# Self-attention of layer 3: partner halves by a VectorE shuffle instead of permutation products

## The reference

```python
cos, sin = _rope_tables(L, x.dtype)                  # L = 32, HEAD_DIM = 16, 16 heads
def _rotate_half(x):
    x1, x2 = (x[..., :HEAD_DIM // 2], x[..., HEAD_DIM // 2:])
    return jnp.concatenate([-x2, x1], axis=-1)
q = q * cos + _rotate_half(q) * sin
k = k * cos + _rotate_half(k) * sin
scores = jnp.einsum('bhqd,bhkd->bhqk', q, k) / sqrt(hd)
out = jnp.einsum('bhqk,bhkd->bhqd', softmax(scores), v)
x = x + out @ o_w.T + o_b                            # q, k, v are projections of the layer norm of x
```

## Time and profile before

| | us |
|---|---|
| median of 3 runs (3510.6 to 3521.19) | 3512.74 |
| profiled execution, its span | 3512.3 |
| of it the self-attention of layer 3, first to last instruction (2203.68 to 2332.94) | 129.3 |
| one turn of its loop | 7.06 |

### The profile page before, as it was taken

One profiled execution on the slowest core, in us unless ns is written; L12 is line 12 of the kernel. 1 busy time (PEld: TensorE's weight loads), 2 busy tenths in 40 slices (PEclk: granted clock), 3 DMA queues, 4 the chain that ended last, 5 costly groups with the idle time before them and its releaser, 6 DMA issues. The chain is left out here.

```text
span 3512.3 us, 105565 instructions
## 1 busy us (share of the span) xinstructions
PE 3266.2 (93%) x39150; PEld 2585.9 (74%) x39150; DVE 2217.2 (63%) x7505; ACT 1454.0 (41%) x4212; POOL 1003.2 (29%) x1620
## 2 busy tenths in 40 slices
PE   7978999999987999999999999888999999988799
PEld 6767887777766888888877777765666777767576
DVE  4767226666667988889556666763334666668455
ACT  2334335555532333333255555541111555556222
POOL 0112113333243444444323333442110111112421
PEclk9989999999997999999999999979999999999699
DMA  6643332222112000000011111042112111110323
GB/s 222 212 177 154 115 100 58 57 57 54 62 40 103 3 2 2 2 2 2 13 44 45 43 43 44 2 146 98 46 46 69 43 39 39 39 35 2 114 79 113
DMA packets 145872, 225.26 MB, mean 64 GB/s; under 512 B 14216, under 2 KB 121480, under 8 KB 143816
## 3 DMA queue, kind: packets, MB, share of 16 engines
q1 hardware_dynamic: 138816, 203.16, 18.4%
q0 software_dynamic: 6816, 18.69, 1.5%
HBM read 201.03 MB, written 38.74 MB: 68 GB/s over the span
## 5 line engine op out<-in xcount | busy, mean ns | idle before, releaser
L3303 POOL TENSOR_TENSOR l1fu_second_weighed<-l1fu_second,l1fu_parts 128x256 bf16<-128x256 bf16 x384 | 273.0, 739 | 342.9 <-DVE l1fu_second L3544 336.0
L3355 PEld LDWEIGHTS l1fu_ps_u<-l1f_xnT_all,l1f_key_in 128*128 128x128 f32 x2048 | 252.5, 195 | 17.4 <-issue 11.2
L3355 PE MATMUL l1fu_ps_u<-l1f_xnT_all,l1f_key_in 128*128 (+1 forms) x2048 | 255.0, 279 | 8.7 <-issue 5.5
L3366 PE MATMUL l1fu_ps_y<-l1f_key_out,l1fu_units 128*128 128x256 f32 x1024 | 250.6, 389 | 1.7 <-DVE l1fu_units L3552 1.7
L3366 PEld LDWEIGHTS l1fu_ps_y<-l1f_key_out,l1fu_units 128*128 128x128 f32 x1024 | 185.7, 190 | 33.3 <-issue 6.0
L3417 ACT COPY l1fu_plane<-l1fu_ps_p 128x512 f32<-128x512 f32 x128 | 75.1, 586 | 249.4 <-PE l1fu_ps_p L3345 249.4
L3539 DVE TENSOR_TENSOR l1fu_first<-l1fu_index,l1fu_counted 128x1024 bf16<-128x1024 bf16 x128 | 165.0, 1289 | 20.3 <-PE l1fu_ps_p L3345 17.6
L3425 ACT ACTIVATE l1fu_units<-l1fu_ps_u 128x512 f32<-128x512 f32 x128 | 76.6, 599 | 150.6 <-PE l1fu_ps_y L3366 138.5
L3011 DVE TENSOR_TENSOR l2f_hidden<-l2f_hidden,l2f_ps_u 128x512 f32<-128x512 f32 x55 | 37.8, 688 | 148.9 <-PE l2f_ps_u L2755 139.1
L1020 ACT ACTIVATE l2x_scores<-l2x_scores,l2x_minus_big 128x257 f32<-128x257 f32 x256 | 129.2, 513 | 2.5 <-DVE l2x_minus_big L1104 2.4
L1020 ACT ACTIVATE l1x_scores<-l1x_scores,l1x_minus_big 128x257 f32<-128x257 f32 x256 | 129.2, 513 | 2.1 <-DVE l1x_minus_big L1104 2.1
(11 more groups left out here) (747 smaller groups left out, 8379.8 us busy)
## 6 DMA issues: line engine op xcount, KB each, us to landing
rows_by_expert<-in_zeros_dram SPq DMA_DIRECT2D x1, 17544.0 KB
l0x_ctxT<-in_ctx_T_dram SPq DMA_DIRECT2D x32, 514.0 KB, 5.2
l0x_ctx_rows<-in_ctx_dram SPq DMA_DIRECT2D x64, 256.0 KB, 3.4
l0f_w<-in_L_ffn_w_dram SPq DMA_DIRECT2D x16, 1024.0 KB, 5.1
l1x_ctx_sb<-in_ctx_T_dram SPq DMA_DIRECT2D x64, 256.0 KB, 2.8
l2x_ctx_sb<-in_ctx_T_dram SPq DMA_DIRECT2D x64, 256.0 KB, 2.8
l3x_ctx_sb<-in_ctx_T_dram SPq DMA_DIRECT2D x64, 256.0 KB, 2.8
l1x_mask_raw<-in_mask_int_dram SPq DMA_DIRECT2D x16, 514.0 KB, 3.9
```

The source lines that it names most:

```text
L3303: last = nc.gpsimd.tensor_tensor(second_weighed[:, k % 2, part], second[:, k % 2], parts[:, 1 - par, part, TC * k:TC * k + TC].unsqueeze(2 ...
L3355: last = nc.tensor.matmul(ps_u[:, k % 2, j, :], key_in[:, c, JS * k + j, :], xnT_all[:, c, bass.ts(tile, P)], start=(c == 0), stop=(c == C ...
L3366: last = nc.tensor.matmul(ps_y, units[:, k, j, :], key_out[:, JS * k + j, :], start=(k + j == 0), stop=(k == K - 1 and j == JS - 1))
```

## The change

The partner halves come from VectorE. Its instruction `stream_shuffle` copies a tile and takes, inside each group of 32 partitions, each output partition from the input partition that a list of 32 names; here p XOR 8. `swap_halves` shuffles `kraw` into `krot` and `qT` into `qrot` at the end of VectorE's turn i, behind `normed`, and signals `rot_ready`, for which `rotate_keys` on GpSimd and `spread_queries` of the next turn wait as before. `rotated`, `keep_rotated`, the bank `ps_qkr` and the matrix `other_half` (64 KB of the table of constants) are gone. The values have their own bank as in the other layers, and the two waits between scores and values are gone.

```diff
-        "other_half": p[:, None] == (p ^ (HD // 2))[None],
...
-        if rope:
-            ps_qkr = ps("ps_qkr", [P, 2, C, P])
-            ps_v = ps_s[:, 0, P:P + D]
-        else:
-            ps_v = ps("ps_v", [P, 512])[:, 0:D]
+        ps_v = ps("ps_v", [P, 512])[:, 0:D]
...
+        other_half = [p ^ (HD // 2) for p in range(32)]
...
             def scores(n, slot):
-                if rope:
-                    pe.wait_ge(s["v_spread"], n)
...
-            def rotated(n, slot):
-                after(pe, s["rot_ready"], n - 1)
-                pe.wait_ge(s["qT_ready"], n)
-                pe.wait_ge(s["kraw_ready"], n)
-                for a, raw in enumerate((qT[:, slot], kraw[:])):
-                    for c in range(C):
-                        last = nc.tensor.matmul(ps_qkr[:, a, c, :], core.table("other_half"), raw[:, c, :], start=True,
-                                                stop=True)
-                last.then_inc(s["qkr_ready"], 1)
...
             def values(n, slot):
-                if rope:
-                    after(pe, scores_read, n - 1)
...
-                if rope and there(i, QA):
-                    rotated(i + QA + 1, (par + QA) % 2)
...
-            def keep_rotated(n):
-                act.wait_ge(s["qkr_ready"], n)
-                after(act, s["kT_ready"], n - 1)
-                after(act, s["q_spread"], n - 1)
-                nc.scalar.copy(rot[:], ps_qkr[:]).then_inc(s["rot_ready"], 1)
...
-                if rope and there(i, QA):
-                    keep_rotated(i + QA + 1)
...
+            def swap_halves(n, slot):
+
+                after(dve, s["kT_ready"], n - 1)
+                wait(dve, s["kraw_ready"], n)
+                nc.vector.stream_shuffle(krot, kraw[:], other_half)
+                after(dve, s["q_spread"], n - 1)
+                wait(dve, s["qT_ready"], n)
+                nc.vector.stream_shuffle(qrot, qT[:, slot], other_half).then_inc(s["rot_ready"], 1)
...
                     normed(dve, nc, s, i + XA + 2, core.x[:, i + XA + 1, :], xn[:], mean[:], rstd[:])
                 if is_turn(i, -XA):
                     fill()
+                if rope and there(i, QA):
+                    swap_halves(i + QA + 1, (par + QA) % 2)
```

More of the change, by code:

```diff
@@ L235, in ps @@
             return ctx.enter_context(nc.psum_tensor(f"{tag}_{name}", shape, F32))
-        s = semaphores(nc, tag, LN_SEMS + """ turned xnT_ready qk_ready qkr_ready v_ready
+        s = semaphores(nc, tag, LN_SEMS + """ turned xnT_ready qk_ready v_ready
             qT_ready kraw_ready rot_ready k_turned kT_ready q_spread v_spread scores_ready biased_ready
```

## The result

Twelve runs of the changed kernel have a median of 3529.26 us, against 3512.59 us for twelve runs of the kernel before beside them. The ratio is 1.0042 with an interval of [1.0029, 1.0054], a loss of 14.8 us (10 to 19). I had put most on no measurable change (0.53) and 0.41 on slower; slower it is. By the ratio on the announced 3512.74 us the time is 3527.5 us, just inside my range of 3511 to 3528; the median itself lies 1.3 us above its top. My own forecast was 9.3 us, 3522. The profiled execution lasts 3527.9 us, 15.6 us more than the one of before.

A forecast was written before the change was run, and what follows sets the result against it. A closed VectorE-TensorE loop was taken as the bound, with TensorE in it only from transposes to output product. Thirteen shuffle pairs at s = 0.88 us, 11.4 us, less 2.1 gave 9.3 us, 3522 us; range 3511 to 3528.

The forecast's parts named there:

- rival A: VectorE's two shuffles don't overlap with neighbours: s = 1.0 to 1.24 us, 3524 to 3527 us; chance 0.32.
- the forecast's own range: With s from 0.64 to 1.0 us and the lag gain up to 0.2 us: 3517 to 3524 us.
- The loop: Third layer's self-attention: a turn is a closed loop over VectorE and TensorE, links summing to 7.08 us.
- D: TensorE, 96% busy in the loop, is the bound: 10 to 13 us come back, about 3501 us; chance 0.05.
- B: Only VectorE's own work counts in the loop: 6.85 us a turn, about -2 us, 3511 us; chance 0.10.
- s: Time the two shuffles put between `xn` and the next reciprocal on VectorE: 0.88 us, bounds 0.64 and 1.24 us.
- The gain of 0.10 us from `mixed` to the transposes: TensorE reaches its waits sooner in the loop: 0.31 to 0.21 us a turn, bounds nothing and 0.2 us.
- 13 s - 2.1: Sum over loop, unrolled turns, tail and constants: 9.3 us slower with s at 0.88 us.
- s - 0.35: Turns before tile 1's: second shuffle pair costs s, but the first scores start some 0.35 us earlier.
- The tail: Turns after the loop: shuffles for tiles 12 and 13 partly absorbed by waiting for TensorE, costing s - 0.6.
- The smaller table of constants: Table 64 KB smaller of 515.5 KB, load of 3.7 us: up to 0.46 us gained, counted as -0.15.
- rival C: TensorE's clock falls to 0.5 as it pauses; 3.5 us from transposes to add double, +35 us or more; chance 0.03.

The follow-up runs named there:

- e1: Changed kernel plus eight unread TensorE products where the permutation products were; 3524.64 us, ratio 1.0045 to the kernel before.
- e11: The kernel with eight unread TensorE products added to the changed kernel, unchanged, measured again on another occasion; 3518.89 us, ratio 1.0028 to the kernel before.
- e4: Kernel before with only the values in their own bank and without the two waits between scores and values; 3515.76 us, ratio 1.0011.
- e10: Changed kernel with shuffles and bias addition behind `mixed`, queries and keys behind TensorE's output product, no unread products; 3508.78 us, ratio 1.0001 to the kernel before.
- e2: Changed kernel without the keys' shuffle, the queries' shuffle cut to two elements; 3522.64 us, ratio 1.0030 to the kernel before.
- e9: Changed kernel with shuffles and GpSimd's bias addition moved behind `mixed`, plus eight unread TensorE products; 3513.15 us, ratio 1.0011 to the kernel before.
- e6: Changed kernel with shuffles moved behind `mixed`, plus eight unread TensorE products; 3517.72 us, ratio 1.0017 to the kernel before.
- e12: The changed kernel again, unchanged, on the chip of e9 and e10; 3524.46 us, ratio 1.0044 to the kernel before.

## Why the prediction was right in part, and what failed

- **The range.** That the time lies in it is luck. Most of its upper part stood there for rival A, dearer shuffles, and the forecast's own range ended at 3524. The shuffles were cheaper than the working value; what carried the time to 3527.5 us was the clock, which the range left out.
- **The loop.** Right. The links of the changed kernel at full clock add up to the measured 7.76 us with the one new link of 0.68 us, the removed products, ScalarE's copy and GpSimd were in no link, and D and B fell: taking TensorE's work away gave nothing back, in e1 putting it back gained.
- **s, 0.88 us.** Mis-sized; it measured 0.68 us, close to the lower bound of 0.64. A shuffle takes 0.44 us, as worked out from the transposes, but the load of the list that I added at 0.07 us costs nothing. Rival A, no overlap, is out with it, though the time lies only just above its 3524 to 3527 us. The estimate from the Trainium skill's "The perf-mode tier table" ("VectorE: DVE Perf Modes"), 0.53 us a shuffle, was further off; the measurement decides.
- **The gain of 0.10 us from `mixed` to the transposes.** Mis-sized, about 0.03 us a turn on the mean of the ten. It was read from one turn, and the lag depends on the parity: in the changed kernel's loop it is 0.31 us in one turn (`mixed` ends at 2256.08, the transposes start at 2256.39) and 0.21 us in the next (2263.84 to 2264.05). Before, the same two turns have 0.31 to 0.35 and 0.25 to 0.28 us. In the written-out turn ahead of the loop it is 0.06 us, before and after.
- **The sum without the clock.** With the measured s, 13 s - 2.1 gives 6.7 us, 3519 us. e1 has the sublayer at 136.2, e11 at 138.9 us, 5.7 and 8.4 us over before. For the loop alone 10 x (0.68 - 0.03) = 6.5 us, and e1 has 77.06 - 70.56 = 6.5 us. For the turns ahead of the first reciprocal the sum had s - 0.35 = 0.33 us; measured is 0.1 us, less than their scatter. The tail absorbed more than said (the four turns behind the loop are 0.6 us shorter than before, not s - 0.6 longer), and e4, which changes the bank of the values alone, has the same 0.6 us there; I had the bank at nothing. The smaller table of constants landed after 3.2 instead of 3.7 us, and the first statistics start at 4.9 instead of 5.2 us, 0.3 us where I had 0.15.
- **The step that failed: the clock, rival C at 0.03.** I priced it as all or nothing, 1.2 GHz for all of the 3.5 us from the transposes to the add in every turn, +35 us, and so rare. It came as 3.3 us at 1.2 GHz in every second turn. A long turn costs 9.28 - 7.65 = 1.63 us (7.65 is the same turn in e1); six of them are 9.8 us. The sublayer then closes: shuffles 0.69 + 6.5, clock 9.8, ahead of the first reciprocal +0.1, the four turns behind the loop -0.6, the rest behind the last reciprocal -1.2: 15.3 us, as measured. The last term is the clock as well: that stretch took 6.04 us at a granted clock of 0.50 before and 4.84 us at 0.90 after, and 4.84 at 0.83 and 6.03 at 0.50 in e1 and e11, which are one kernel. So it is no gain of the change. I had seen the two pauses of 1 us and had the row with a clock of 0.70, and I weighed it against one stretch at 1.00, picked from another sublayer. The Trainium skill, "TensorE: Matmul & The Clock Gate", Part 1, says that "the default state is throttled, and activity releases the throttle"; e1 agrees, since work that nobody reads brought the clock from 0.82 in every second turn to 1.00 in all.

Open: which pauses suffice. e10 pauses too (0.34 ahead of the transposes, 0.38 ahead of the output product, 0.33 to 0.39 ahead of the scores) and stays at 1.00; e1 has one pause of 1.1 us and stays at 1.00; e2 has 1.2 us ahead of the scores in nearly every turn and, ahead of the transposes, 0.4 us in five turns and 0.9 us in four, and falls in three. More than this the runs do not show, and not why some turns of e2 fall and others like them don't. Open too is the remainder of several totals: e1, e4 and e9 lie some 5 to 10 us above what their sublayers explain. Most of the scatter from profile to profile is in the first sublayer, which no edit touches and which took 223 to 235 us, so for any effect under 10 us I draw on the sublayer's time and not on a total, and for one under 3 us on the loop's.

## What to carry to other kernels

When work is taken off TensorE in a loop that another engine closes, write down the pauses that it leaves and read the granted clock in single turns of the nearest stretch with such pauses; the saved work can cost more than it took. An operation that is added to an engine belongs behind that engine's own signal to the loop, where it waits anyway (e9: both shuffles for nothing). And where an instruction moves in time, look at what GpSimd does beside it: one row of 0.86 us among rows of 0.42 us is a collision.

## What the runs showed of the hardware

- A shuffle of 128x256 f32 takes 0.43 to 0.46 us and is followed after 0.33 to 0.34 us; over 2 elements 0.16 us, followed after 0.07 us, in the turns of 7.38 to 7.42 us after 0.40 to 0.45 us. The load of its list is a row of 0.01 us with the same start.
- TensorE's clock alternated from turn to turn: 0.82 and 1.00 over stretches of 9.3 and 7.8 us, projections at 3.38 and 1.95 us, and unread products with 0.97 us of weight loads a turn ended it.
- A VectorE multiplication with two inputs in SBUF takes 0.86 us instead of 0.42 us when a GpSimd addition of 128x256 runs beside it.
- TensorE's transposes start 0.05 to 0.15 us after `mixed` in the written-out turn 1; in each pass of the hardware loop it is 0.31 to 0.36 us in the first turn and 0.20 to 0.28 us in the second (before, changed, e1, e4, e6, e9, e10 and e12). What the difference comes from was not tried.
